# Four rounds of a gate and up step in another order, and PSUM banks divided by reader

## What is computed

```python
def dequant(q, s, g=128):            # W[o, i] = q[o, i] * s[o, i // g]
    ...
gate_score = silu(einsum('bsh,ih->bsi', x, Wg))       # x: [2, 512 -> tokens, 512], Wg, Wu: [1792, 512]
intermediate = gate_score * einsum('bsh,ih->bsi', x, Wu)
return einsum('bsi,hi->bsh', intermediate, Wd)        # Wd: [512, 1792]
```

## Time and profile before

| | |
|---|---|
| median of 3 runs | 1949.75 us (1949.33 to 1951.79) |
| the profiled execution | 1946.96 us, its span 1945.0 us |
| TensorE busy | 1910.1 us, 98% |
| TensorE weight loads | 1553.2 us, 80% |
| ScalarE busy | 1621.2 us, 83% |
| VectorE busy | 1538.5 us, 79% |
| GpSimd busy | 1510.3 us, 78% |
| the rounds (L1105, first and last start) | 190.1 to 353.0 us |

### The profile page before, as it was taken

One profiled execution on the slowest core, in us unless ns is written; L12 is line 12 of the kernel. 1 busy time (PEld: TensorE's weight loads), 2 busy tenths in 40 slices (PEclk: granted clock), 3 DMA queues, 4 the chain that ended last, 5 costly groups with the idle time before them and its releaser, 6 DMA issues.

```text
span 1945.0 us, 32828 instructions
## 1 busy us (share of the span) xinstructions
PE 1910.1 (98%) x10675; PEld 1553.2 (80%) x10675; DVE 1538.5 (79%) x2790; ACT 1621.2 (83%) x3272; POOL 1510.3 (78%) x1102
## 2 busy tenths in 40 slices
PE   8999999999999999999999999999999999999998
PEld 6574767777888888888888888888888888888876
DVE  8787899966787877777877777777787878787878
ACT  5354877658898989898989898989898998989896
POOL 5644667646888888888888888888788888888887
PEclk9999999999999999999999999999999999999999
DMA  5615323553343434333343343434343433343333
GB/s 209 197 60 147 111 87 103 160 181 104 122 120 119 125 117 123 125 107 125 107 131 112 120 123 109 124 108 138 102 137 108 133 109 124 121 158 118 119 104 125
DMA packets 114474, 241.74 MB, mean 124 GB/s; under 512 B 23681, under 2 KB 24706, under 8 KB 113794
## 3 DMA queue, kind: packets, MB, share of 16 engines
q1 hardware_dynamic: 110466, 227.06, 36.9%
q0 software_dynamic: 3840, 12.59, 2.3%
HBM read 226.75 MB, written 12.85 MB: 123 GB/s over the span
## 4 chain that ended last, share of the span: by engine, by line
PE 76%; DVE 1%; issue 1%; ACT 1%; POOL 0%; DVEq 0%; ACTq 0%; POOLq 0%
PE ps L75 21%; PE ps L77 20%; PE ps L76 20%; PE ps L2130 6%; PE ps L2138 4%; PE ps L2077 3%; PE ps L2061 1%; PE ps L2120 0%; DVE s_y_lo L2565 0%; PE ps L2069 0%; POOL w_lo L2729 0%; DVE g_stage L2718 0%; DVE xs L1945 0%; ACT s_y_hi L2272 0%; ACT s_lm L2215 0%
## 5 line engine op out<-in xcount | busy, mean ns | idle before, releaser
L75 PE MATMUL ps<-h_hi,w_hi 128*128 128x512 f32 x1168 | 477.5, 409 | 2.7 <-POOL w_hi L890 1.6
L2729 POOL TENSOR_TENSOR w_lo<-w_raw,w_hi 128x1024 fp32r<-128x1024 f32 x142 | 338.4, 2392 | 157.7 <-ACT w_hi L2198 157.7
L2477 DVE SCALAR_TENSOR_TENSOR s_cv<-ps,s_par,s_cv 128x511 f32<-128x511 f32 (+2 forms) x480 | 357.6, 748 | 125.9 <-ACT s_cv L2248 113.6
L76 PE MATMUL ps<-h_lo,w_hi 128*128 128x512 f32 x1168 | 457.1, 391 | 0.0
L77 PE MATMUL ps<-h_hi,w_lo 128*128 128x512 f32 x1152 | 451.5, 392 | 0.0
L2755 POOL TENSOR_TENSOR s_lm<-s_lm,s_cbt 128x512 f32<-128x512 f32 x256 | 327.8, 1306 | 12.5 <-ACT s_lm L2230 10.4
L2215 ACT ACTIVATE s_lm<-s_rows,s_steps 128x128 f32<-128x128 f32 x1024 | 324.5, 390 | 14.1 <-PE ps L2130 14.1
L75 PEld LDWEIGHTS ps<-h_hi,w_hi 128*128 128x128 f32 x1168 | 220.1, 188 | 55.2 <-issue 11.4
L77 PEld LDWEIGHTS ps<-h_hi,w_lo 128*128 128x128 f32 x1152 | 216.5, 188 | 48.5
L76 PEld LDWEIGHTS ps<-h_lo,w_hi 128*128 128x128 f32 x1168 | 220.6, 189 | 39.6 <-issue 0.2
L75 PE MATMUL ps<-s_wo_hi,s_y_hi 128*128 128x512 f32 x512 | 203.8, 398 | 3.3 <-DVE s_y_lo L2565 3.3
(11 more groups left out here) (339 smaller groups left out, 4419.7 us busy)
## 6 DMA issues: line engine op xcount, KB each, us to landing
w_raw<-in_w_in SPq DMA_DIRECT2D x144, 512.0 KB, 3.8
s_rows<-acs_dram SPq DMA_DIRECT2D x256, 256.0 KB, 3.5
s_wo_raw<-in_w_out SPq DMA_DIRECT2D x128, 256.0 KB, 3.3
w_raw<-in_gu_q SPq DMA_DIRECT2D x14, 512.0 KB, 3.7
f_d_q<-in_d_q SPq DMA_DIRECT2D x28, 256.0 KB, 2.7
f_d_w<-in_d_s SPq DMA_DIRECT2D x28, 256.0 KB, 3.5
table<-shifted SPq DMA_DIRECT2D x16, 256.0 KB, 3.0
xs<-in_x SPq DMA_DIRECT2D x8, 256.0 KB, 6.2
```

What stands on the lines that cost most here:

```text
L75: nc.tensor.matmul(dst, l_hi, r_hi, start=start, stop=False)
L76: nc.tensor.matmul(dst, l_hi, r_lo, start=False, stop=False)
L2477: nc.vector.scalar_tensor_tensor(dst, src[:, 0:SEQ - d], par[:, v.b, 4 * j + 3 - d:4 * j + 4 - d], dst, ALU.mult, ALU.add).then_inc(conv_c ...
L2729: nc.gpsimd.tensor_tensor(w_lo[:, slot, :], w_raw[:, slot, :], w_hi[:, slot, :].bitcast(F32), ALU.subtract).then_inc(w_lo_ready, 1)
```

## The change

The order of the rounds in a half becomes 0, 2, 1, 3, and the bank pair of a round becomes k // 2: rounds 0 and 1, which ScalarE empties, use banks 0 and 1; rounds 2 and 3, which VectorE empties, use banks 2 and 3. The waits follow. The down tiles keep their places between the rounds, with tile 2 ahead of tile 1. ScalarE's and VectorE's own orders stay, but for step 0, half 0, where ScalarE takes round 1 at the third of the four input tiles, not at the second.

```diff
+ROUNDS = (0, 2, 1, 3)
@@ pe_group
-                if k >= 2:
-                    pe.wait_ge(group_scaled, 4 * h + 2 * (k - 2) + part + 1)
+                took = group_added if k >= 2 else group_scaled
+                if k % 2:
+                    pe.wait_ge(took, 4 * h + part + 1)
                 elif h:
-                    pe.wait_ge(group_added, 4 * (h - 1) + 2 * k + part + 1)
+                    pe.wait_ge(took, 4 * (h - 1) + 2 + part + 1)
...
-                dst = ps[:, 2 * (k % 2) + part, :]
+                dst = ps[:, 2 * (k // 2) + part, :]
@@ pe_gate_up
-                for k in range(KD):
+                for k in ROUNDS:
@@ act_group
-                act.wait_ge(group_done, 8 * h + 2 * k + part + 1)
+                act.wait_ge(group_done, 8 * h + 2 * ROUNDS.index(k) + part + 1)
...
-                nc.scalar.activation(dst, ps[:, 2 * (k % 2) + part, :], ACT.Copy,
+                nc.scalar.activation(dst, ps[:, 2 * (k // 2) + part, :], ACT.Copy,
@@ dve_groups
-                    dve.wait_ge(group_done, 8 * h + 2 * k + part + 1)
+                    dve.wait_ge(group_done, 8 * h + 2 * ROUNDS.index(k) + part + 1)
                     dve.wait_ge(group_scaled, 4 * h + 2 * (k - 2) + part + 1)
-                    nc.vector.scalar_tensor_tensor(dst, ps[:, 2 * (k % 2) + part, :], gu_s[:, m, part, k:k + 1], dst,
+                    nc.vector.scalar_tensor_tensor(dst, ps[:, 2 * (k // 2) + part, :], gu_s[:, m, part, k:k + 1], dst,
@@ TensorE's program, step 0
-                    pe_group(pe, 0, 0, t)
+                    pe_group(pe, 0, 0, ROUNDS[t])
...
-            for k in range(KD):
+            for k in ROUNDS:
                 pe_group(pe, 0, 1, k)
@@ ScalarE's program, step 0
-                if t < 2:
-                    act_group(act, 0, 0, t)
+                if t in (0, 2):
+                    act_group(act, 0, 0, t // 2)
```

## The result

The changed kernel takes 1973.74 us (median of 4 runs, 1972.04 to 1975.27) beside 1950.03 us for the kernel before: ratio 1.0120 with a 95% interval of [1.0108, 1.0132]. It is 23.7 us slower. The prediction said slower by 15.5 us, 1965 in a range of 1958 to 1971. The direction and the moved wait were right, but the time lies outside the range: the sum had too little for the granted clock and for the end of the stage. The profiled execution took 1972.89 us, its span 1970.8.

The account below looks back on a forecast made before the run. TensorE, busy 98%, bounds the kernel; steps with extra VectorE work are VectorE's. 5.14 + 1.1 + 1.4 + 7.6 + 0.25 = 15.5 us on the median 1949.75 gives 1965.2, forecast 1965, range 1958 to 1971.

Parts of the forecast that it names:

- The moved wait: TensorE's wait for VectorE leaves half 0's first place for half 1's fourth (places: rounds in TensorE's order), 1.62 us forward.
- The faster rival: VectorE's round 2 of half 1 (t: its start) is done when TensorE reaches the fourth place: 1944 us, chance 0.04.
- The loop, 11.07 and 12.87: Step length from t to t: 11.07 us without extras against 10.23, 12.87 with them (scans) against 12.02.
- steps 5 to 13: Nine steps each lose 0.85 us at the moved wait: +7.6 us, bounds 4.5 and 10.
- Step 0, without the clock: Half 1's fourth place waits for VectorE's round 2, dt product behind it: +5.14 us with the 0.66, bounds 3.5 and 6.5.
- +0.66 for the later turned tiles: Step 0: ScalarE's round 1 behind the third xn tile makes the last turned tiles late: +0.66 us, bounds 0 and 1.3.
- Steps 2 to 4: Steps with extras, TensorE also held by ScalarE's queue: 37.8 us for 36.42, +1.4, bounds -0.7 and +3.
- The clock, "+1.1, bounds 0 and 1.6": Step 0: after about 5 us standing still, 5 dt matmuls at half clock, +0.23 us each: +1.1.
- up to 2.7 at the fourth place with extras: In steps with extra VectorE passes, TensorE's wait at half 1's fourth place lasts up to 2.7 us.
- The end, "+0.25, bounds 0 and 0.6": After step 13, down stage starts 1.8 us later than the shift, but GpSimd's chain only 0.25 later: +0.25.
- The layer's end: Sign in the changed kernel's profile: the layer ends near 421 us instead of 405.7.
- The rival "dearer": Clock falls again in long-wait steps or in_lo collides with GpSimd's add: half a microsecond more a step, +22, 1972; chance 0.10.

Follow-up runs that it names:

- half1_new: Changed kernel with the new round order kept only in half 1 of steps 1 to 13, old order elsewhere; ratio to the kernel before 1.0095.
- queue: Changed kernel with step 0 in old order and VectorE doing round 2 of half 1 before scale_down, extras and product; ratio to the kernel before 0.9993.
- fill: Changed kernel plus 18 matmuls nobody reads, issued in step 0 ahead of the fourth place of half 1; ratio to the kernel before 1.0109, paired 1.0112.
- after_paired: Changed kernel timed again, with down tiles going by place, tile 1 ahead of tile 2; ratio to the kernel before 1.0125.
- last_old: Changed kernel with the old round order in half 1 of step 13 only; one execution, stage 243.44 us, no ratio.
- dt_ahead: Changed kernel with step 0's dt product issued before the fourth place of half 1; ratio to the kernel before 1.0095.
- half0_from3: Changed kernel with the new order only in half 0 of steps 3 to 13, old order elsewhere; 1944.08 against 1945.94 us, ratio 0.9985.

## Why the prediction was right in direction and too small

- **The moved wait.** Right, and the base of everything: at the fourth place of half 1 in every step, for VectorE's round 2, and at no first place. half1_new and queue show it from both sides. The faster rival needed t early enough; t never was (TensorE had waited 0.28 us even in step 9, the shortest).
- **The loop, 11.07 and 12.87.** Measured 11.09 and 12.86. Take one fall of the clock (12.53 - 11.09 = 1.4) from the +9.17 of steps 5 to 13, and +7.7 stays against 7.6. The scale_down (1.79) and the slow product (1.36) kept their length, as priced: VectorE's and GpSimd's overlap moved with the loop. The Trainium skill ("SBUF — State Buffer", section "SBUF: two separate sides") says that VectorE and GpSimd take turns on a shared port pair, for a whole instruction each. It would have given time back had the shift parted the two; by the same lengths before and after, it didn't.
- **Step 0, without the clock.** The mechanism and 4.48 of the 5.14 between t of step 0 and step 1 were right (fill: 4.49). The +0.66 for the later turned tiles was right too: after_paired, whose slow stretch at the layer's start was as short as before's, had t0 at 18.07 (+0.66). In the first trace that start ran longer at half clock (TensorE had stood 7.36 us, not 3.24), which is the other +1.0; it comes from what lies ahead of the stage and is chance.
- **Steps 2 to 4.** +1.07 against +1.4, within its bounds.
- **The clock, "+1.1, bounds 0 and 1.6".** The first step that failed. It was mis-sized, 2.6 where it stood (2.2 and 1.2 in other executions): the prediction took 5 slow matmuls, and the granted clock stayed at 0.50 for the whole stretch from 213 to 217 us. And it was counted once: another fall came in step 7, +1.4, behind a wait of 2.18 us, for which the prediction had up to 2.7 at the fourth place with extras, but put the fall into a rival. Together 4.0 for 1.1. The Trainium skill ("TensorE: Matmul & The Clock Gate", section "Why this matters for your kernels") warns of longer idle gaps than that one. Here the granted clock dropped behind it all the same (0.56 from 307.50 to 311.30).
- **The end, "+0.25, bounds 0 and 0.6".** The second step that failed, and the larger: +3.53, so 3.3 too little. Here the path was wrong, and not only a size. The prediction held that TensorE's late start of the down stage would be hidden, since GpSimd's chain, on which that stage waits, would be only 0.25 later than the shift. But that chain runs through TensorE: the last down tile stood behind the very wait that was priced at 1.8, and ScalarE's in_hi, a place later, added 0.88 to it. last_old shows the sum as 3.2. The layer's end came near 431.2 us, and not 421: 7.0 of that is the stage and 3.0 the chance ahead of it.

The differences by term are 1.0, 1.5, -0.3, 1.6 and 3.3: together 7.0, from 15.5 to 22.5. The rival "dearer" (1972, with a chance of 0.10) named the second fall of the clock, and its 1972 is 1.7 below the median. But most of its +22 came from half a microsecond more in every step, which didn't come (11.09 for 11.07), and it had nothing for the end. That its time was near is luck.

**What stays open.** Whether filling the wait of step 0, or using it, brings more falls in steps 5 to 7 (3 in both traces of fill, 2 in dt_ahead, 1 in the three traces of the changed kernel), or whether that is chance: last_old, which is the changed kernel up to step 13, had 2 as well. And whether those falls would stop if the waits of about 2 us there were filled: that wasn't tried; queue shows only that with those waits gone there were none.

## What to carry to other kernels

A wait that is moved to another place in an engine's queue has the price of what is queued behind it there: look for the producer's place in its own queue first, then for useful work that can go ahead of the wait, and follow the last iteration by itself, since its neighbours are others. When a change creates waits of about 2 us on TensorE in one step after another, put falls of the clock into the sum as a term with bounds, and not only into a rival. Try a reordering on each half by itself: here one half won 0.4 us in the steps that wait for VectorE, and the other alone lost 1.25 in every step from 4 on (11.47 for 10.22, 13.26 for 12.02, falls of the clock left out).

## What the runs showed of the hardware

- The granted clock fell behind waits of 1.7 to 2.6 us, not only behind standstills of 3 to 5. In the nine profiled executions that had the new order in half 1 with its wait, there were one to three falls at the fourth place of steps 5 to 7, where the waits were longest (1.73, 2.18 and 2.18 in the first trace, up to 2.58 in half1_new); in the five without that wait there was none. A wait of that length is not enough by itself: the first trace has one of 2.18 in step 6 with no fall behind it, and queue one of 2.16 (253.10 above). Which step had it varied: step 7 in the first trace, step 6 in the second of the same kernel, though the wait was 2.18 or 2.17 in both steps of both.
- A fall cost 1.2 to 1.6 us in a step (14.42 for 12.86, 12.53 for 11.09, 14.45 for 13.26), 1.2 to 2.6 behind the wait of step 0, and at most 0.4 in the down stage (64.80 to 65.17 with it, 64.75 and 64.83 without).
- Some of VectorE's instructions with two operands in SBUF took longer beside GpSimd's: in_lo 1.80 us for 0.68 (half0_from3), the product 1.35 for 0.66. Its sums from PSUM took 0.73 to 0.76 us with GpSimd at work and without. Which of two that start together is the one to be lengthened can differ between steps of one execution: in half0_from3 it was GpSimd's add (1.88 for 1.30) in the other late steps, and in_lo in one.
- The begin of the stage varied by 11 us (188.58 to 199.79) between executions, in code that no edit touched. That is half of what was to be measured. An account within the stage is free of it, but for the first stretch, where the clock at the begin differs.
